# Rounding the transposed probabilities of a wide row tile in one piece instead of two

## The chip, the cores and the metric

The kernel runs on one core of a Trainium2 chip. The metric is the device time of one execution in microseconds. A core has TensorE (PE; its weight loads are the rows PEld), VectorE (DVE), ScalarE (ACT), GpSimd (POOL) and SyncE (SP), each with its own queue of instructions, and they wait for each other by semaphores. PSUM, into which PE writes, has eight banks of 512 fp32 columns.

## What is computed

One transformer layer with attention and a gated feed-forward part side by side, cut to what matters here:

```python
xn = _layernorm(x)                                  # x: 2 x 1024 x 256
q = (xn @ Wq + bq).reshape(b, h, t, dh)             # 16 heads of 128
k = (xn @ Wk + bk).reshape(b, t, h, dh).transpose(0, 2, 3, 1)
v = (xn @ Wv + bv).reshape(b, t, h, dh).transpose(0, 2, 1, 3)
logits = jnp.einsum('bhtd,bhds->bhts', q, k) * scale
mask = jnp.triu(jnp.full((t, t), -jnp.inf, dtype=x.dtype), k=1)
weights = jax.nn.softmax(logits + mask, axis=-1)
out = jnp.einsum('bhts,bhsd->bhtd', weights, v)
attn = out.transpose(0, 2, 1, 3).reshape(b, t, h * dh) @ Wo + bo
result = x + attn + ffn(xn)                         # ffn: 4-bit weights, 2048 wide
```

## The kernel before

All products are made to near fp32 precision from two fp32r parts, a rounded high part and a rest: `split_matmul` (lines 41 to 43) issues three matmuls, high by high, high by low, low by high. So each operand that comes out of PSUM is first rounded by ScalarE (`..._hi`) and then subtracted by VectorE (`..._lo`).

The norm and the feed-forward part come first. Then follows a loop over 256 row tiles `s`: 32 heads (two sequences of 16) times 8 row tiles of 128 queries. By the causal mask row tile `i` of a head has `i + 1` blocks of 128 keys. Its stages are:

- PE: the scores into one of two bank pairs (banks 0-1, 2-3), `scores(s)`.
- DVE, line 858: adds the mask, moves the scores to `probs` and makes the row maximum. ACT, line 420: the exponential. POOL, lines 635 and 638: one over the row sum, and the scaling of `probs`.
- three tiles later (`LAG`), PE, line 1029: transposes the `i + 1` blocks of `probs` into bank 5 or 6, four blocks to a bank. Tiles 4 to 7 are wide: they take two banks, in two chunks. ACT, line 406 (`pt_high`): rounds a chunk into `pt_hi`. DVE, line 770 (`pt_low`): subtracts into `pt_lo`. A head has 12 chunks, which take bank 5 and 6 in turn, and a chunk's transposes wait until the chunk before the last one is subtracted:

```python
wait(pe, pt_lo_done, at - 1)
```

- PE, `with_v`: the product of two row tiles with V, into bank 4, every second step.

Between these stages each step has jobs of K, V and output projections, which all use bank 7 (`M`), one after the other. A job waits until DVE has emptied bank 7 of the job before it (`job_lo_done`): lines 723 (K), 728 (V), 735 (output). For K and V ACT first makes the high part (lines 384, 387). The order is written out in tables, the same for all heads:

```python
FIRST_AT = {0: "K0", 2: "O0a", 6: "O1b", 7: "Vb"}
EARLY_AT = {1: "K1", 3: "O0b", 5: "O1a"}
LATE_AT = {3: "Va"}
```

In step `i` PE does the transposes of the tile three steps back, the FIRST job, the scores of tile `i`, the EARLY job, the product with V where `i` is odd, and the LATE job. So the transposes of tiles 3, 4, 5, 6, 7 of a head stand in steps 6, 7, 0, 1, 2, and those of the next head's tile 0 in step 3. Between the transposes of tile 7 and of tile 0 stand O0a and the scores of tile 2 only; between those of tiles 5 and 6 K0 and the scores of tile 0. DVE does in step `i`: `pt_low` of the tile three back, the FIRST job's evacuation, line 858, the EARLY job's. In step 2 it does O0a's output sum between the two chunks of tile 7. In heads 7, 15 and 23 the steps 2 to 6 also project Q for the next eight heads (`q_step`).

Of the kernel before, what the change touches and what calls it, by code (L numbers as in the profile page):

```python
# [14 lines left out]
ACT = mybir.ActivationFunctionType  # L15
# [3 lines left out]
P = 128  # L19
# [15 lines left out]
def flat(ap):  # L35
    return ap.rearrange("p a b -> p (a b)")
# [9 lines left out]
def wait(eng, sem, count):  # L46

    if count > 0:
        eng.wait_ge(sem, count)
# [6 lines left out]
def attention(nc, sh, d, out):  # L56
# [4 lines left out]
    GROUP = N // (SEQ // HEADS)  # L61
    GROUPS = NH // GROUP
    TILES = SEQ // P
    CHUNKS = 12
    QT = N // P
    QUARTER = 2 * P
    LAG = 3
# [6 lines left out]
    ps, ident = sh["ps"], sh["ident"]  # L74
# [2 lines left out]
    flat_acc = flat(sh["acc"][:])  # L77
    S = [ps[:, 0:2, :], ps[:, 2:4, :]]
    O, M = ps[:, 4, :], ps[:, 7, :]
    T = [ps[:, 5, :], ps[:, 6, :]]  # L80
    D = [ps[:, 4, :], ps[:, 5, :]]
    WT = flat(ps[:, 6:8, :])[:, 0:W6]

    with ExitStack() as c:
# [84 lines left out]
        def job_of(h, name):  # L169

            if name is None:
                return None
            if name[0] == "K":
                return ("K", h + 1, int(name[1])) if h + 1 < NH else None
            if name[0] == "V":
                pair, j = (h + 1) // 2, (0 if h % 2 else 2) + "ab".index(name[1])
                return ("V", pair, j) if pair < NH // 2 else None
            return ("O", h - 1, int(name[1]), "ab".index(name[2])) if h > 0 else None
# [4 lines left out]
        nth = {job: k + 1 for k, job in enumerate(ORDER)}  # L183
        nth_hi = {job: k + 1 for k, job in enumerate(j for j in ORDER if j[0] != "O")}

        chunk_of = lambda i: i if i < QT else 2 * i - QT
        banks_of = lambda i: 1 if i < QT else 2
        chunk_no = lambda s, ch: s // TILES * CHUNKS + chunk_of(s % TILES) + ch
        pt_block = lambda q: 0 if q % 2 == 0 else 6
        new_group = lambda h: h % GROUP == GROUP - 1 and h + 1 < NH  # L190
        q_steps = lambda h, i: Q_AFTER.get(i, ()) if new_group(h) else ()
# [128 lines left out]
        def _(act):  # L320
# [77 lines left out]
            def pt_high(s):  # L398

                i = s % TILES  # L400
                for ch in range(banks_of(i)):
                    at = chunk_no(s, ch)
                    blocks = min(QT, i + 1 - ch * QT)
                    act.wait_ge(pt_done, at + 1)
                    first = pt_block(i // 2) + ch * QT
                    nc.scalar.activation(  # L406
                        pt_hi[:, first:first + blocks, i % 2 * P:(i % 2 + 1) * P],
                        T[at % 2][:, 0:blocks * P].rearrange("p (a b) -> p a b", b=P), ACT.Copy
                    ).then_inc(pt_hi_done, 1)

            def o_high(h, half):
                act.wait_ge(pv_done, 4 * h + 2 * half + 2)
# [239 lines left out]
        def _(dve):  # L652
# [106 lines left out]
                    dve.wait_ge(q_lo_done, 2 * GROUP * o)  # L759
                q_evacuate(o, u)  # L760

            def pt_low(s, ch):

                i = s % TILES
                at = chunk_no(s, ch)
                blocks = min(QT, i + 1 - ch * QT)
                dve.wait_ge(pt_hi_done, at + 1)
                first = pt_block(i // 2) + ch * QT
                where = (slice(None), slice(first, first + blocks), slice(i % 2 * P, (i % 2 + 1) * P))
                nc.vector.tensor_tensor(pt_lo[where], T[at % 2][:, 0:blocks * P].rearrange("p (a b) -> p a b", b=P),  # L770
                                        pt_hi[where].bitcast(F32), ALU.subtract).then_inc(pt_lo_done, 1)

            def o_low(h, half):
# [65 lines left out]
            dve.wait_ge(mask_made, 1)  # L839
            for s in range(NH * TILES):  # L840
                h, i = divmod(s, TILES)
                between = FIRST_AT.get(i) == "O0a"
                if i - 1 in LATE_AT:
                    evacuate(job_of(h, LATE_AT[i - 1]))
                if s >= LAG:
                    pt_low(s - LAG, 0)
                    if between:
                        evacuate(job_of(h, FIRST_AT[i]))
                    if banks_of((s - LAG) % TILES) > 1:
                        pt_low(s - LAG, 1)  # L850
                if not between or s < LAG:
                    evacuate(job_of(h, FIRST_AT.get(i)))
                hurry = EARLY_AT.get(i) == "O1a"
                if hurry:
                    evacuate(job_of(h, EARLY_AT[i]))
                dve.wait_ge(scores_done, s + 1)
                width = (i + 1) * P
                nc.vector.tensor_tensor_reduce(  # L858
                    probs[:, s % 4, 0:width], flat(bank_of("S", h, i))[:, 0:width], mask_row[:, SEQ - width:SEQ],
                    -1.0, -MASKED, ALU.add, ALU.min, neg_max[:, s % 16:s % 16 + 1]).then_inc(max_done, 1)  # L860
                if not hurry:
                    evacuate(job_of(h, EARLY_AT.get(i)))
                if i == 3 and h > 0:
                    o_low(h - 1, 1)
                if i == 7:
                    o_low(h, 0)
                if i == 1 and new_group(h):
                    wq_low((h + 1) // GROUP * HEADS)
                    wq_low((h + 1) // GROUP * HEADS + 1)
                for u in q_steps(h, i):  # L870
                    q_step(h // GROUP + 1, u)

            def pt_lows(s):
                for ch in range(banks_of(s % TILES)):
                    pt_low(s, ch)

            end = NH * TILES
            pt_lows(end - 3)
            evacuate(("O", NH - 1, 0, 0))
            pt_lows(end - 2)  # L880
            evacuate(("O", NH - 1, 0, 1))
            pt_lows(end - 1)
            o_low(NH - 1, 1)
            evacuate(("O", NH - 1, 1, 0))
            evacuate(("O", NH - 1, 1, 1))
# [2 lines left out]
        def _(pe):  # L888
# [130 lines left out]
            def transposes(s):  # L1019
                i = s % TILES  # L1020
                pe.wait_ge(probs_done, s + 1)
                if s == 0:
                    pe.wait_ge(acc_done, STEPS)
                for ch in range(banks_of(i)):
                    at = chunk_no(s, ch)
                    wait(pe, pt_lo_done, at - 1)
                    for n in range(min(QT, i + 1 - ch * QT)):
                        b = ch * QT + n
                        last = nc.tensor.transpose(T[at % 2][:, n * P:(n + 1) * P], probs[:, s % 4, b * P:(b + 1) * P],  # L1029
                                                   ident[:])  # L1030
                    last.then_inc(pt_done, 1)

            def with_v(h, q):

                pe.wait_ge(pt_lo_done, chunk_no(h * TILES + 2 * q + 1, banks_of(2 * q + 1) - 1) + 1)
                pe.wait_ge(job_lo_done, nth[("V", h // 2, q)])
                if q % 2 == 0:
                    wait(pe, o_lo_done, 2 * h + q // 2)
                for s in range(2 * q + 2):
                    first = P if s == 2 * q + 1 else 0  # L1040
                    out_ = O[:, q % 2 * QUARTER + first:(q % 2 + 1) * QUARTER]
                    b = pt_block(q) + s
                    last = split_matmul(nc, out_, v_hi[:, h % VSLOTS, s, :], v_lo[:, h % VSLOTS, s, :],
                                        pt_hi[:, b, first:], pt_lo[:, b, first:], s == 0, s == 2 * q + 1)
                last.then_inc(pv_done, 1)
# [111 lines left out]
```

## Time and profile before

| | |
|---|---|
| median of 3 runs | 1270.23 us (1269.38 to 1271.47) |
| the profiled execution | 1270.06 us |
| its span, first to last instruction | 1268.3 us |
| mean granted TensorE clock | 0.995 |
| PE busy | 1236.2 us (97%), 8306 matmuls |
| PEld busy | 1119.3 us (88%) |
| DVE busy | 876.2 us (69%) |
| ACT busy | 738.6 us (58%) |
| POOL busy | 737.8 us (58%) |
| the transposes, line 1029 | 1152, 172.5 us busy, PE idle before them 2.6 us |
| `pt_hi`, line 406 | 384 operations, 174.2 us busy |
| `pt_lo`, line 770 | 384 operations, 204.0 us busy |

The loop over the heads runs from about 342 us to the end. Busy times are sums over the whole execution. The end of a matmul is modelled, so for PE the starts are the sharper reading. An engine's idle time is charged to what released it.

### The profile page before, as it was taken

The numbers are of one execution on the slowest core, as the hardware profiler recorded it, in microseconds if no ns is written. First come the engines' busy times: TensorE is split into PE (matmuls) and PEld (weight loads), VectorE is DVE, ScalarE is ACT, GpSimd is POOL, SyncE is SP. The second block draws the span as 40 slices with busy tenths as digits, with TensorE's granted clock in tenths as the row PEclk, the third lists the DMA queues.
The fourth block names the chain that finished last, engine by engine and source line by source line (L and its number), as shares of the span: only waits on it lengthen the run. The fifth ranks groups of instructions, "written<-read, shape, count | busy, mean of one in ns | idle before, by whom it ended". The sixth has DMA issues, their size and how long they took to land.

```text
span 1268.3 us, 22067 instructions
## 1 busy us (share of the span) xinstructions
PE 1236.2 (97%) x8306; PEld 1119.3 (88%) x8306; DVE 876.2 (69%) x1694; ACT 738.6 (58%) x1533; POOL 737.8 (58%) x772
## 2 busy tenths in 40 slices
PE   8899999999999999999999999999999999999997
PEld 6688888888899999879999998899999879999996
DVE  7687777776577766667667776677667666677765
ACT  3444444444466666657666675566666656666663
POOL 5574455443376676626666663476775527666663
PEclk9999999999999999999999999999999999999999
DMA  5200000000000000110000002010000100000001
GB/s 143 46 14 13 11 10 14 26 2 9 9 26 13 15 13 18 40 49 13 14 26 5 22 13 72 14 55 13 13 22 10 47 26 14 18 22 7 12 5 34
DMA packets 57337, 29.96 MB, mean 24 GB/s; under 512 B 16272, under 2 KB 57232, under 8 KB 57232
## 3 DMA queue, kind: packets, MB, share of 16 engines
q1 hardware_dynamic: 56016, 27.62, 7.9%
q8 instruction: 68, 1.11, 0.4%
q10 hardware_dynamic: 1216, 0.93, 0.2%
q14 instruction: 37, 0.30, 0.1%
HBM read 26.44 MB, written 2.10 MB: 22 GB/s over the span
## 4 chain that ended last, share of the span: by engine, by line
PE 84%; DVE 5%; ACT 4%; POOL 3%; issue 2%; DMA 1%; SPq 1%; ACTq 0%; POOLq 0%; DVEq 0%
PE ps L41 26%; PE ps L43 25%; PE ps L42 25%; PE ps L1029 8%; DVE k_lo L723 2%; ACT k_hi L384 2%; ACT q_all L335 1%; DMA raw<-in_down 1%; PE ps L922 1%; POOL acc L572 1%; DVE pt_lo L770 0%; POOL codes L551 0%; DVE probs L858 0%; DMA wq_in<-in_wq 0%; POOL w_rows L563 0%
## 5 line engine op out<-in xcount | busy, mean ns | idle before, releaser
L635 POOL TENSOR_TENSOR inv_sum<-row_sum,minus_one 128x1 f32<-128x1 f32 x256 | 141.0, 551 | 309.5 <-ACT probs L420 307.7
L638 POOL TENSOR_TENSOR probs<-probs,inv_sum 128x128 f32<-128x128 f32 (+7 forms) x256 | 296.5, 1158 | 20.0
L770 DVE TENSOR_TENSOR pt_lo<-ps,pt_hi 128x512 fp32r<-128x512 f32 (+3 forms) x384 | 204.0, 552 | 97.5 <-ACT pt_hi L406 97.4
L420 ACT ACTIVATE probs<-probs,neg_max 128x128 f32<-128x128 f32 (+7 forms) x256 | 198.1, 774 | 61.2 <-DVE neg_max L858 58.4
L406 ACT ACTIVATE pt_hi<-ps 128x512 fp32r<-128x512 f32 (+3 forms) x384 | 174.2, 489 | 85.2 <-PE ps L1029 85.2
L858 DVE CUSTOM_DVE_ANT_0 probs<-ps,mask_row 128x128 f32<-128x128 f32 (+7 forms) x256 | 192.1, 751 | 2.6
L42 PE MATMUL ps<-pt_lo,v_hi 128*128 128x256 f32 (+1 forms) x640 | 180.1, 281 | 0.0
L43 PE MATMUL ps<-pt_hi,v_lo 128*128 128x256 f32 (+1 forms) x640 | 180.0, 281 | 0.0
L1029 PE MATMUL ps<-ident,probs 128*128 128x128 f32 x1152 | 172.5, 277 | 2.6 <-DVE pt_lo L770 1.9
L41 PE MATMUL ps<-pt_hi,v_hi 128*128 128x256 f32 (+1 forms) x640 | 173.2, 271 | 1.6 <-DVE pt_lo L770 1.6
L618 POOL TENSOR_TENSOR hid_lo<-act_buf,hid_hi 128x512 fp32r<-128x512 f32 x64 | 82.7, 1293 | 147.0 <-ACT hid_hi L359 147.0
L41 PE MATMUL ps<-k_hi,q_hi 128*128 128x512 f32 (+3 forms) x384 | 140.6, 366 | 0.0
L1029 PEld LDWEIGHTS ps<-ident,probs 128*128 128x128 f32 x1152 | 127.3, 140 | 11.0 <-POOL probs L638 2.8
L43 PE MATMUL ps<-k_hi,q_lo 128*128 128x512 f32 (+3 forms) x384 | 132.9, 346 | 0.0
L42 PE MATMUL ps<-k_lo,q_hi 128*128 128x512 f32 (+3 forms) x384 | 132.7, 346 | 0.0
L41 PEld LDWEIGHTS ps<-pt_hi,v_hi 128*128 128x128 f32 x640 | 121.8, 190 | 4.4 <-DVE pt_lo L770 1.8
L42 PEld LDWEIGHTS ps<-pt_lo,v_hi 128*128 128x128 f32 x640 | 121.8, 190 | 2.7
L43 PEld LDWEIGHTS ps<-pt_hi,v_lo 128*128 128x128 f32 x640 | 122.1, 191 | 0.0
L455 ACT ACTIVATE act_buf<-ps 128x512 f32<-128x512 f32 x64 | 38.4, 599 | 140.4 <-PE ps L43 140.4
L775 DVE SCALAR_TENSOR_TENSOR o_lo<-ps,bv,o_hi 128x512 fp32r<-128x512 f32 x64 | 48.1, 751 | 102.5 <-ACT o_hi L413 102.5
L41 PE MATMUL ps<-xn_hi,w_hi 128*128 128x512 f32 x256 | 103.3, 403 | 0.9 <-DVE w_lo L703 0.4
L42 PE MATMUL ps<-xn_lo,w_hi 128*128 128x512 f32 x256 | 101.8, 398 | 0.0
(105 smaller groups left out, 3211.8 us busy)
## 6 DMA issues: line engine op xcount, KB each, us to landing
wq_in<-in_wq SPq DMA_DIRECT2D x63, 128.0 KB, 2.3
kv_in<-in_wk SPq DMA_DIRECT2D x16, 256.0 KB, 2.8
wo_in<-in_wo SPq DMA_DIRECT2D x32, 128.0 KB, 2.0
kv_in<-in_wv SPq DMA_DIRECT2D x32, 128.0 KB, 2.3
out<-acc SPq DMA_DIRECT2D x8, 256.0 KB, 2.6
acc<-in_x SPq DMA_DIRECT2D x2, 512.0 KB, 5.0
raw<-in_gate SPq DMA_DIRECT2D x16, 64.0 KB, 1.8
raw<-in_up SPq DMA_DIRECT2D x16, 64.0 KB, 2.1
```

The lines of the kernel that those rows point to most:

```text
L41: nc.tensor.matmul(out, w_hi, m_hi, start=start, stop=False)
L42: nc.tensor.matmul(out, w_hi, m_lo, start=False, stop=False)
L43: return nc.tensor.matmul(out, w_lo, m_hi, start=False, stop=stop)
L406: nc.scalar.activation(pt_hi[:, first:first + blocks, i % 2 * P:(i % 2 + 1) * P], T[at % 2][:, 0:blocks * P].rearrange("p (a b) -> p a b", ...
L420: nc.scalar.activation(probs[:, s % 4, 0:width], probs[:, s % 4, 0:width], ACT.Exp, bias=neg_max[:, s % 16:s % 16 + 1], scale=-1.0, accum_ ...
L618: nc.gpsimd.tensor_tensor(hid_lo[:, k % 4, :], act_buf[:, k % 4, :], hid_hi[:, k % 4, :].bitcast(F32), ALU.subtract).then_inc(hid_lo_done, 1)
L635: nc.gpsimd.tensor_tensor(inv_sum[:, at], row_sum[:, at], minus_one[:], ALU.pow).then_inc(inv_done, 1)
L638: nc.gpsimd.tensor_tensor(row, row, inv_sum[:, at].to_broadcast([P, (i + 1) * P]), ALU.mult).then_inc(probs_done, 1)
L770: nc.vector.tensor_tensor(pt_lo[where], T[at % 2][:, 0:blocks * P].rearrange("p (a b) -> p a b", b=P), pt_hi[where].bitcast(F32), ALU.subt ...
L775: nc.vector.scalar_tensor_tensor(o_lo[:], O, bv[:, h % HEADS:h % HEADS + 1], o_hi[:].bitcast(F32), ALU.add, ALU.subtract).then_inc(o_lo_do ...
L858: nc.vector.tensor_tensor_reduce(probs[:, s % 4, 0:width], flat(bank_of("S", h, i))[:, 0:width], mask_row[:, SEQ - width:SEQ], -1.0, -MASK ...
L1029: last = nc.tensor.transpose(T[at % 2][:, n * P:(n + 1) * P], probs[:, s % 4, b * P:(b + 1) * P], ident[:])
```

## The change

A row tile's transposes are one piece. A wide tile fills banks 5 and 6 together, and ScalarE and VectorE each handle its `i + 1` blocks (640 to 1024 columns) in one operation over both banks. A narrow tile takes bank 5 or 6 by the parity of `s`. `pt_done`, `pt_hi_done` and `pt_lo_done` count row tiles instead of chunks. A tile that is wide, or that follows a wide one, waits until the tile before it is subtracted as a whole (`t_free`); the others wait for the tile before that. Nothing else is changed; DVE's sum of O0a, having no place between two chunks any more, follows `pt_low`.

```diff
-    CHUNKS = 12
...
-    T = [ps[:, 5, :], ps[:, 6, :]]
+    T = ps[:, 5:7, :]
...
-        chunk_of = lambda i: i if i < QT else 2 * i - QT
         banks_of = lambda i: 1 if i < QT else 2
-        chunk_no = lambda s, ch: s // TILES * CHUNKS + chunk_of(s % TILES) + ch
+        t_bank = lambda s: flat(T) if banks_of(s % TILES) > 1 else T[:, s % 2, :]
+        t_free = lambda s: s if banks_of(s % TILES) > 1 or banks_of((s - 1) % TILES) > 1 else s - 1
...
             def pt_high(s):
 
                 i = s % TILES
-                for ch in range(banks_of(i)):
-                    at = chunk_no(s, ch)
-                    blocks = min(QT, i + 1 - ch * QT)
-                    act.wait_ge(pt_done, at + 1)
-                    first = pt_block(i // 2) + ch * QT
-                    nc.scalar.activation(
-                        pt_hi[:, first:first + blocks, i % 2 * P:(i % 2 + 1) * P],
-                        T[at % 2][:, 0:blocks * P].rearrange("p (a b) -> p a b", b=P), ACT.Copy
-                    ).then_inc(pt_hi_done, 1)
+                act.wait_ge(pt_done, s + 1)
+                first = pt_block(i // 2)
+                nc.scalar.activation(
+                    pt_hi[:, first:first + i + 1, i % 2 * P:(i % 2 + 1) * P],
+                    t_bank(s)[:, 0:(i + 1) * P].rearrange("p (a b) -> p a b", b=P), ACT.Copy).then_inc(pt_hi_done, 1)
...
-            def pt_low(s, ch):
+            def pt_low(s):
 
                 i = s % TILES
-                at = chunk_no(s, ch)
-                blocks = min(QT, i + 1 - ch * QT)
-                dve.wait_ge(pt_hi_done, at + 1)
-                first = pt_block(i // 2) + ch * QT
-                where = (slice(None), slice(first, first + blocks), slice(i % 2 * P, (i % 2 + 1) * P))
-                nc.vector.tensor_tensor(pt_lo[where], T[at % 2][:, 0:blocks * P].rearrange("p (a b) -> p a b", b=P),
+                dve.wait_ge(pt_hi_done, s + 1)
+                first = pt_block(i // 2)
+                where = (slice(None), slice(first, first + i + 1), slice(i % 2 * P, (i % 2 + 1) * P))
+                nc.vector.tensor_tensor(pt_lo[where], t_bank(s)[:, 0:(i + 1) * P].rearrange("p (a b) -> p a b", b=P),
                                         pt_hi[where].bitcast(F32), ALU.subtract).then_inc(pt_lo_done, 1)
...
-                between = FIRST_AT.get(i) == "O0a"
                 if i - 1 in LATE_AT:
                     evacuate(job_of(h, LATE_AT[i - 1]))
                 if s >= LAG:
-                    pt_low(s - LAG, 0)
-                    if between:
-                        evacuate(job_of(h, FIRST_AT[i]))
-                    if banks_of((s - LAG) % TILES) > 1:
-                        pt_low(s - LAG, 1)
-                if not between or s < LAG:
-                    evacuate(job_of(h, FIRST_AT.get(i)))
+                    pt_low(s - LAG)
+                evacuate(job_of(h, FIRST_AT.get(i)))
...
                 pe.wait_ge(probs_done, s + 1)
                 if s == 0:
                     pe.wait_ge(acc_done, STEPS)
-                for ch in range(banks_of(i)):
-                    at = chunk_no(s, ch)
-                    wait(pe, pt_lo_done, at - 1)
-                    for n in range(min(QT, i + 1 - ch * QT)):
-                        b = ch * QT + n
-                        last = nc.tensor.transpose(T[at % 2][:, n * P:(n + 1) * P], probs[:, s % 4, b * P:(b + 1) * P],
-                                                   ident[:])
-                    last.then_inc(pt_done, 1)
+                wait(pe, pt_lo_done, t_free(s))
+                for b in range(i + 1):
+                    last = nc.tensor.transpose(t_bank(s)[:, b * P:(b + 1) * P], probs[:, s % 4, b * P:(b + 1) * P], ident[:])
+                last.then_inc(pt_done, 1)
 
             def with_v(h, q):
 
-                pe.wait_ge(pt_lo_done, chunk_no(h * TILES + 2 * q + 1, banks_of(2 * q + 1) - 1) + 1)
+                pe.wait_ge(pt_lo_done, h * TILES + 2 * q + 2)
```

The engines' queues show two places. VectorE, steps 1 and 2 of a head: `pt_lo` of tiles 6 and 7, the maxima (line 858) of tiles 1 and 2, `k_lo` of K1, and `acc`, the output sum of O0a. Before:

```order
L770 TENSOR_TENSOR pt_lo<-ps,pt_hi 128x4x128 [waits pt_hi_done]
L770 TENSOR_TENSOR pt_lo<-ps,pt_hi 128x3x128 [waits pt_hi_done]
L858 ISA probs,neg_max<-ps,mask_row 128x256 [waits scores_done]
L858 ISA neg_max 128x1
L723 SCALAR_TENSOR_TENSOR k_lo<-ps,bk,k_hi 128x512 [waits job_hi_done]
L770 TENSOR_TENSOR pt_lo<-ps,pt_hi 128x4x128 [waits pt_hi_done]
L735 TENSOR_TENSOR acc<-ps,acc 128x512 [waits job_done]
L770 TENSOR_TENSOR pt_lo<-ps,pt_hi 128x4x128 [waits pt_hi_done]
L858 ISA probs,neg_max<-ps,mask_row 128x384 [waits scores_done]
```

The same place in the changed kernel (its line numbers are its own):

```order
L763 TENSOR_TENSOR pt_lo<-ps,pt_hi 128x7x128 [waits pt_hi_done]
L845 ISA probs,neg_max<-ps,mask_row 128x256 [waits scores_done]
L845 ISA neg_max 128x1
L718 SCALAR_TENSOR_TENSOR k_lo<-ps,bk,k_hi 128x512 [waits job_hi_done]
L763 TENSOR_TENSOR pt_lo<-ps,pt_hi 128x8x128 [waits pt_hi_done]
L730 TENSOR_TENSOR acc<-ps,acc 128x512 [waits job_done]
L845 ISA probs,neg_max<-ps,mask_row 128x384 [waits scores_done]
```

The pairs are one operation each, and the output sum has moved from between the two halves of tile 7 to behind the whole.

TensorE, steps 2 and 3: the transposes of tile 7, O0a (lines 41 to 43 with `wo`), the scores of tile 2 (with `k`), the transpose of the next head's tile 0, the scores of tile 3. Before:

```order
L1029 MATMUL ps<-ident,probs 128x128 [waits pt_lo_done,probs_done]
L1029 MATMUL ps<-ident,probs 128x128 x3
L1029 MATMUL ps<-ident,probs 128x128 [waits pt_lo_done]
L1029 MATMUL ps<-ident,probs 128x128 x3
L41 MATMUL ps<-wo_hi,o_hi 128x256 [waits o_lo_done,wo_lo_done,job_lo_done]
...
L43 MATMUL ps<-k_hi,q_lo 128x384
L1029 MATMUL ps<-ident,probs 128x128 [waits pt_lo_done,probs_done]
L41 MATMUL ps<-k_hi,q_hi 128x512 [waits max_done]
```

In the changed kernel:

```order
L1009 MATMUL ps<-ident,probs 128x128 [waits pt_lo_done,probs_done]
L1009 MATMUL ps<-ident,probs 128x128 x7
L41 MATMUL ps<-wo_hi,o_hi 128x256 [waits o_lo_done,wo_lo_done,job_lo_done]
...
L43 MATMUL ps<-k_hi,q_lo 128x384
L1009 MATMUL ps<-ident,probs 128x128 [waits pt_lo_done,probs_done]
L41 MATMUL ps<-k_hi,q_hi 128x512 [waits max_done]
```

PE's order is unchanged. The wait in the middle of tile 7 is gone, and the `pt_lo_done` that tile 0 waits for is that of all of tile 7, where it was that of its first four blocks.

## Rows read from the trace of the kernel before

**Rows 1.** Windows: span, busy (x) of PE, PEld, DVE, ACT, POOL; PEclk, DMA, GB/s

```profile
400.00:1250.00 850.00, 839.10 (x5913) 772.18 (x5911) 585.12 (x1190) 548.51 (x1187) 527.32 (x588) 1.00 0.08 22
```

**Rows 2.** The page, chain of work that ended last, shares by engine

```profile
PE 84%; DVE 5%; ACT 4%; POOL 3%; issue 2%; DMA 1%; SPq 1%; ACTq 0%; POOLq 0%; DVEq 0%
```

**Rows 3.** Waits of PEld, 400 to 1250 us: total us, times, longest us

```profile
PEld ps L41 <- DVE k_lo L723: 7.6, 28, 0.3
```

**Rows 4.** Timeline of PE, transposes, two heads: start us, us, engine, line, op, tiles

```profile
602.50 1.06 PE L1029 MATMUL ps<-ident,probs 128*128 128x128 f32 x8
...
604.63 0.30 PE L1029 MATMUL ps<-ident,probs 128*128 128x128 f32 x1
...
628.84 1.06 PE L1029 MATMUL ps<-ident,probs 128*128 128x128 f32 x8
...
630.97 0.30 PE L1029 MATMUL ps<-ident,probs 128*128 128x128 f32 x1
```

**Rows 5.** Timeline of ACT, evacuations of the transposes, same head

```profile
603.16 1.09 ACT L406 ACTIVATE pt_hi<-ps 128x512 fp32r<-128x512 f32 x2 [0.32 <-PE ps L1029]
...
604.96 0.28 ACT L406 ACTIVATE pt_hi<-ps 128x128 fp32r<-128x128 f32 x1 [0.41 <-PE ps L1029]
...
615.02 0.60 ACT L406 ACTIVATE pt_hi<-ps 128x512 fp32r<-128x512 f32 x1 [0.52 <-PE ps L1029]
```

**Rows 6.** Timeline of DVE, the same place

```profile
603.79 0.69 DVE L770 TENSOR_TENSOR pt_lo<-ps,pt_hi 128x512 fp32r<-128x512 f32 x1 [1.70 <-ACT pt_hi L406]
604.40 0.68 DVE L735 TENSOR_TENSOR acc<-ps,acc 128x512 f32<-128x512 f32 x1
```

**Rows 7.** Timeline of PEld and DVE, weight loads, and what the second waited for

```profile
604.60 0.14 PEld L1029 LDWEIGHTS ps<-ident,probs 128*128 128x128 f32 x1
...
625.27 0.19 PEld L41 LDWEIGHTS ps<-xn_hi,kv_hi 128*128 128x128 f32 x1 [0.27 <-DVE k_lo L723]
...
624.47 0.75 DVE L723 SCALAR_TENSOR_TENSOR k_lo<-ps,bk,k_hi 128x512 fp32r<-128x512 f32 x1 [0.38 <-ACT k_hi L384]
```

**Rows 8.** Groups by line and form: ..., xcount | busy us, mean ns | idle before

```profile
L406 ACT ACTIVATE pt_hi<-ps 128x512 fp32r<-128x512 f32 x192 | 111.0, 596 | 53.4 <-PE ps L1029 53.4
...
L406 ACT ACTIVATE pt_hi<-ps 128x128 fp32r<-128x128 f32 x64 | 17.6, 276 | 11.6 <-PE ps L1029 11.6
...
L770 DVE TENSOR_TENSOR pt_lo<-ps,pt_hi 128x512 fp32r<-128x512 f32 x192 | 132.1, 688 | 90.5 <-ACT pt_hi L406 90.5
...
L770 DVE TENSOR_TENSOR pt_lo<-ps,pt_hi 128x128 fp32r<-128x128 f32 x64 | 18.2, 284 | 2.0 <-ACT pt_hi L406 2.0
```

**Rows 9.** Timeline of PE and DVE, transposes of tiles 3 and 4

```profile
614.36 0.62 PE L1029 MATMUL ps<-ident,probs 128*128 128x128 f32 x4
...
616.76 0.71 PE L1029 MATMUL ps<-ident,probs 128*128 128x128 f32 x5
...
615.66 0.69 DVE L770 TENSOR_TENSOR pt_lo<-ps,pt_hi 128x512 fp32r<-128x512 f32 x1 [0.18 <-ACT pt_hi L406]
```

**Rows 10.** Timeline of PE and DVE, transposes of tiles 5 and 6

```profile
621.48 0.84 PE L1029 MATMUL ps<-ident,probs 128*128 128x128 f32 x6
...
623.90 0.96 PE L1029 MATMUL ps<-ident,probs 128*128 128x128 f32 x7
...
623.08 1.01 DVE L770 TENSOR_TENSOR pt_lo<-ps,pt_hi 128x512 fp32r<-128x512 f32 x2
```

**Rows 11.** Timeline of PE, tiles 7 and 0, in a head that also projects Q

```profile
523.76 1.06 PE L1029 MATMUL ps<-ident,probs 128*128 128x128 f32 x8
...
528.68 0.27 PE L1029 MATMUL ps<-ident,probs 128*128 128x128 f32 x1
```

**Rows 12.** Timeline of PE and windows, two idle times and the clock after one

```profile
58.07 1.41 PE L922 MATMUL ps<-ident,w_rows 128*128 128x128 f32 x6 [3.33 <-issue]
...
58.20:61.60 3.40, 3.40 (x12) 2.92 (x12) 1.37 (x3) 0.00 (x0) 1.00 (x1) 0.50 0.00 0
...
539.84 0.50 PE L41 MATMUL ps<-xn_hi,wq_hi 128*128 128x512 f32 x1 [1.23 <-DVE q_all L750]
```

More of the change, by code:

```diff
@@ L871, in _ @@
                     q_step(h // GROUP + 1, u)
-            def pt_lows(s):
-                for ch in range(banks_of(s % TILES)):
-                    pt_low(s, ch)
             end = NH * TILES
-            pt_lows(end - 3)
+            pt_low(end - 3)
             evacuate(("O", NH - 1, 0, 0))
-            pt_lows(end - 2)
+            pt_low(end - 2)
             evacuate(("O", NH - 1, 0, 1))
-            pt_lows(end - 1)
+            pt_low(end - 1)
             o_low(NH - 1, 1)
```

## The prediction

> **What bounds the kernel now.** I read the windows first: between 400 and 1250 us, all of it the loop over the heads, TensorE is busy 839.1 of 850 us at full granted clock, while VectorE has 585, ScalarE 549 and GpSimd 527 [rows 1]. The chain that ended last agrees: 84% of it is PE [rows 2]. So removing work from ScalarE or VectorE shortens nothing by itself, and only some 11 us of 850 are PE waiting. Of these the largest regular piece is K's second half, which waits until VectorE has emptied the first half out of bank 7: 7.6 us in 28 waits [rows 3]. What remains to read is whether PE's new waits end later than PE gets to them. For that I laid the timelines of PE, ACT and DVE over each other at the four places where transposes follow a wide tile, and at the one where a wide tile follows tile 3.
>
> A head takes 26.34 us (628.84 - 602.50, the same row one head later), and the transposes of tile 0 follow those of tile 7 by 2.13 us in both heads [rows 4]. What holds at one head thus repeats at the others.
>
> **Tile 7 to tile 0: the cost.** Before, tile 0's transpose needed only the first four blocks of tile 7 out of bank 5 or 6. ScalarE begins them at 603.16, while PE still transposes the other four [rows 5]; VectorE subtracts them from 603.79 to 604.48 [rows 6]; PE loads the weights of tile 0 at 604.60 [rows 7], straight after the scores and without a wait. Now it needs all eight blocks. Step by step:
> - ScalarE cannot begin before the last transpose. One transpose lets it begin 0.33 us after PE's start (604.96 - 604.63), four let it begin 0.66 us after (615.02 - 614.36) [rows 4, 5, 9]: 0.11 us each. Eight: 0.33 + 7 x 0.11 = 1.10, so 602.50 + 1.10 = 603.60. ScalarE has nothing else then; it idled 0.32 us before 603.16.
> - The rounding of 1024 columns: 128 columns take 276 ns, 512 take 596 [rows 8], so 107 ns per 128 and 276 + 7 x 107 = 1.02 us: until 604.62. VectorE begins 0.03 us behind (603.79 against 603.76): 604.65.
> - The subtraction: 284 and 688 ns [rows 8], 135 ns per 128, 284 + 7 x 135 = 1.23 us: until 605.88.
> - PE's weight load follows such a release by 0.05 us (625.27 against 624.47 + 0.75) [rows 7]: 605.93 against 604.60, a stall of 1.33 us. The first products after a stall also come without weights loaded ahead; I add 0.07, as an estimate. I take **1.40 us**.
>
> Bounds: below, 1.25, if a two-bank operation is a little cheaper than the line through its sizes; above, 1.65, if it costs as two operations end to end (1.09 us on ScalarE, 2 x 0.69 less the overlap on VectorE) plus a full reload.
>
> How often: 31 heads are followed by another. In three of them (before heads 7, 15 and 23) Q's projection of the next group stands between the two tiles, and PE gets to tile 0 4.92 us after tile 7 [rows 11], later than the 3.43 it would now have to wait for. That leaves 28: 28 x 1.40 = **39.2 us** (35 to 46). It lies on PE, and PE is the path.
>
> VectorE's output sum O0a moves behind the whole subtraction, from 604.40 to about 605.8. It frees bank 7 for O0b, at about 606.5; PE gets there after tile 0 and scores 3, at about 606.8. It costs nothing now, but its cover is 0.3 us.
>
> **Tile 5 to tile 6.** Transposes at 621.48 [rows 10], ScalarE from 621.48 + 0.33 + 5 x 0.11 = 622.36, 768 columns 0.81 us, VectorE from 623.20 for 0.96, to 624.16, PE's load at 624.21. Its matmuls began at 623.90, so 0.34 us are lost. But right behind them stands the wait for k_lo, and PE idled 0.27 us there [rows 7]; that wait hangs on K's first half, which PE did before tile 6 and which doesn't move. So 0.07 us remain: 31 x 0.07 = **2.2 us** (0 to 10.5, the latter if nothing is absorbed).
>
> **The other places.** Tile 3 to 4: the new wait is for tile 3's subtraction, over at 616.35; PE comes at 616.76 [rows 9]. Nothing, covered by 0.4 us. Tiles 4 to 5 and 6 to 7 have V's or K's projection between them and, for the latter, an attention product besides; I count nothing. At the ends of the loop there is less between the tiles; behind the last tile 7 the product with V waits for the subtraction directly. By the two stalls above I put **1.5 us** there (0.8 to 2).
>
> **What goes.** 128 operations of ScalarE and of VectorE: their fixed part is 276 - 107 = 169 ns and 284 - 135 = 149 ns, so 21.6 and 19.1 us of busy time. On the path they are worth nothing, since both engines idle before these very groups [rows 8]. The Trainium skill (Perfetto Trace Analysis, Optimizing Scalar/DVE Operations) says that grouping pays "if the engine is saturated", and that where these engines are not saturated but cause bubbles elsewhere, breaking instructions up may let work finish sooner. Here the busy shares say the second case. By the first the time would fall, which is the second rival.
>
> **The sum.** 39.2 + 2.2 + 1.5 = 42.9 us on the profiled execution's 1270.06: **1313 us**. That execution lies 0.17 us under the median of the three runs, so it needs no correction.
>
> **The rivals.**
> 1. More is passed on. O0b's cover of 0.3 us is the thinnest: it is gone if the pair of operations takes 0.3 us more than I say, for O0a's sum stands directly behind them. Another 0.3 us in each of 28 heads is 8.4: 1321; with tile 5's 10.5 less 2.2 on top, 1330. For it: VectorE's queue at this place has no idle time left. Against it: the maxima run three tiles ahead of the transposes.
> 2. Not slower. The fixed costs saved let ScalarE and VectorE empty K's first half earlier, and the wait for k_lo (7.6 us) goes: 1262.5. This needs the subtraction of all eight blocks to be over by 604.55, 0.95 us after the last transpose; two operations in a row of 0.60 and 0.69 us for half the width speak against it. Here also belongs the reading in which grouping as such pays: the 20 us of fixed cost would give 1250.
> 3. Part of the stall is given back, because work of the other engines catches up while PE stands and later waits shrink. All that there is to win back is PE's idle 10.9 us: 1302.
> 4. The clock. After PE had idled 3.33 us, the granted clock was 0.50 for 3.4 us, the lower level of 1.2 GHz; after the 1.23 us idle before 539.84 it stayed at 1.00 [rows 12, 1]. Were each of the 28 stalls followed by such a stretch, it would cost 1.7 us each time: 48 more, 1361. The Trainium skill (TensorE: Matmul & The Clock Gate, A second HAM failure mode) tells of a kernel whose short idles at its PSUM buffers make the clock swing between its two levels, which would be this case. The trace so far speaks against it.
>
> **How the numbers follow.** Forecast as summed 0.75; rival 1 0.11, rival 2 0.03, rival 3 0.07, rival 4 0.04. The forecast's own bounds are 1270 + 35 + 0 + 0.8 = 1306 and 1270 + 46 + 10.5 + 2 = 1328, both ends unlikely together; I keep 1303 to 1326. That leaves out rivals 2, 3 and 4 (0.14), the upper part of rival 1 and the outermost of the forecast. A measurement can tell 0.2% or 2.5 us from no change. Faster has rival 2, 0.03; the same 0.01, for a stall found almost wholly covered; slower 0.96.
>
> **What would show it.** PE should wait on pt_lo some 28 times, 1.3 to 1.4 us each, and a head should take 27.7 to 27.8 us instead of 26.34. Two-bank operations should last 1.02 and 1.23 us. The wait for k_lo should almost vanish, and a wait before tile 6 of about 0.3 us stand in its place. ScalarE and VectorE should show about 20 us less work. The granted clock should stay at 1.00. The prediction is wrong if the head stays within 0.3 us of 26.34, if the stall stands at another pair of tiles, or if the clock falls.

## The result, and the profile after

| | before | changed |
|---|---|---|
| median | 1270.29 us | 1316.13 us |
| profiled execution | 1270.06 us | 1317.51 us |
| its span | 1268.3 us | 1315.7 us |
| `pt_hi` operations, busy | 384, 174.2 us | 256, 167.0 us |
| `pt_lo` operations, busy | 384, 204.0 us | 256, 193.5 us |

The kernel became slower. The ratio of its time to that of before is 1.0352, with a 95% interval of 1.0337 to 1.0366, which is 44.7 us (42.8 to 46.5). One disturbed execution of the changed kernel (and one of the run with scores and O0b ahead of tile 0, below) is left out of the ratio but stands in the median; the other three took 1314.25 to 1317.51 us (there 1283.01 to 1285.32).

First the windows, over the same stretch of the head loop as [rows 1], and over one head (from one tile 7 to the next); the columns are those of [rows 1]:

```profile
400.00:1250.00 850.00, 803.33 (x5661) 738.39 (x5660) 553.07 (x1022) 520.83 (x1022) 502.43 (x559) 1.00 0.08 22
```
```profile
642.90:670.70 27.80, 26.22 (x194) 24.47 (x194) 18.26 (x34) 17.38 (x34) 17.86 (x21) 1.00 0.06 16
```

PE idles 46.7 us of 850 where it idled 10.9, at the same granted clock. A head takes 27.80 us instead of 26.34, and PE is idle in 1.58 of them. The page's chain of work that ended last shows what took PE's share ([rows 2] had PE at 84%, ACT at 4% and DVE at 5%):

```profile
PE 77%; ACT 8%; DVE 8%; issue 3%; POOL 2%; DMA 1%; SPq 1%; ACTq 0%; POOLq 0%; DVEq 0%
PE ps L43 22%; PE ps L42 22%; PE ps L41 22%; PE ps L1009 9%; DVE pt_lo L763 5%; ACT pt_hi L402 4%; ACT o_hi L408 2%; ACT q_all L334 1%; DMA raw<-in_down 1%; PE ps L905 1%; POOL acc L567 1%; DMA wq_in<-in_wq 0%; POOL codes L546 0%; DVE probs L845 0%; POOL w_rows L558 0%
```

`pt_hi` and `pt_lo`, which were hidden, now stand in the chain with 9% of the span. The waits of PE and of its weight loads, 400 to 1250 us:

```profile
PE ps L1009 <- DVE pt_lo L763: 39.1, 52, 1.3
...
PEld ps L1009 <- POOL probs L633: 37.0, 24, 1.5
PEld ps L1009 <- issue: 12.1, 28, 0.4
```

The 52 waits are 24 of 1.25 us before tile 0 and 28 of 0.3 us before tile 6. The second line is the same long wait seen at the weight load. That instruction waits for two semaphores, and the record names POOL's `probs`; but those were scaled 3.3 us before the load, and the matmul's own row names `pt_lo`. The wait for `k_lo` of [rows 3] is no longer in the list.

One head's step 2 and 3, from the timelines of PE, PEld, ACT and DVE, answers to [rows 4 to 7]:

```profile
642.91 1.06 PE L1009 MATMUL ps<-ident,probs 128*128 128x128 f32 x8
...
646.44 0.30 PE L1009 MATMUL ps<-ident,probs 128*128 128x128 f32 x1 [1.26 <-DVE pt_lo L763]
```
```profile
646.40 0.14 PEld L1009 LDWEIGHTS ps<-ident,probs 128*128 128x128 f32 x1 [1.55 <-POOL probs L633]
```
```profile
644.00 1.03 ACT L402 ACTIVATE pt_hi<-ps 128x1024 fp32r<-128x1024 f32 x1 [1.28 <-PE ps L1009]
```
```profile
645.07 1.22 DVE L763 TENSOR_TENSOR pt_lo<-ps,pt_hi 128x1024 fp32r<-128x1024 f32 x1 [2.55 <-ACT pt_hi L402]
646.21 0.68 DVE L730 TENSOR_TENSOR acc<-ps,acc 128x512 f32<-128x512 f32 x1
646.80 0.55 DVE L845 CUSTOM_DVE_ANT_0 probs<-ps,mask_row 128x384 f32<-128x384 f32 x1
```

Measured from the first transpose of tile 7, tile 0 starts 3.53 us after it, where it was 2.13. ScalarE starts 1.09 us after it and works 1.03; VectorE starts 0.04 behind and works 1.22; its end at 646.29 is followed by PE's load 0.11 later.

Tiles 5 and 6 of the next head, where PE waits for the whole of tile 5 ([rows 10] had 2.42 us between them; here it is 2.83):

```profile
663.26 0.84 PE L1009 MATMUL ps<-ident,probs 128*128 128x128 f32 x6
...
666.09 0.96 PE L1009 MATMUL ps<-ident,probs 128*128 128x128 f32 x7 [0.32 <-DVE pt_lo L763]
```

I subtracted, over all heads, the distance between the starts of neighbouring tiles' transposes in the trace of before from that in the trace after. Tile 7 to tile 0 takes 1.40 us more in 28 pairs and 0.0 in the other three, 39.2 us together. Tile 5 to 6 takes 0.41 more in all 32 heads, 13.2 us, and tile 6 to 7 0.33 less in 30 of them, -10.2 us. The other pairs sum to 1.2. Ahead of the loop there are 1.8 us more, and behind the last transposes of tile 7 2.3; both are looked at in the last section.

### The profile page after: what moved, and what is told of

It is laid out like the page before. It is cut to its first block, busy times and chain, and to the rows that moved or that the text cites. A ratio compares the mean times of both kernels' runs of the same rounds, so it can differ in the third digit from the quotient of the medians.

```text
span 1315.7 us, 21811 instructions
## 1 busy us (share of the span) xinstructions
PE 1236.6 (94%) x8306; PEld 1119.6 (85%) x8306; DVE 871.2 (66%) x1566; ACT 734.4 (56%) x1405; POOL 736.8 (56%) x772
## 4 chain that ended last, share of the span: by engine, by line
PE 77%; ACT 8%; DVE 8%; issue 3%; POOL 2%; DMA 1%; SPq 1%; ACTq 0%; POOLq 0%; DVEq 0%
PE ps L43 22%; PE ps L42 22%; PE ps L41 22%; PE ps L1009 9%; DVE pt_lo L763 5%; ACT pt_hi L402 4%; ACT o_hi L408 2%; ACT q_all L334 1%; DMA raw<-in_down 1%; PE ps L905 1%; POOL acc L567 1%; DMA wq_in<-in_wq 0%; POOL codes L546 0%; DVE probs L845 0%; POOL w_rows L558 0%
## 5 line engine op out<-in xcount | busy, mean ns | idle before, releaser
L763 DVE TENSOR_TENSOR pt_lo<-ps,pt_hi 128x128 fp32r<-128x128 f32 (+7 forms) x256 | 193.5, 756 | 141.5 <-ACT pt_hi L402 139.9
L402 ACT ACTIVATE pt_hi<-ps 128x128 fp32r<-128x128 f32 (+7 forms) x256 | 167.0, 652 | 131.1 <-PE ps L1009 130.7
L613 POOL TENSOR_TENSOR hid_lo<-act_buf,hid_hi 128x512 fp32r<-128x512 f32 x64 | 82.7, 1292 | 148.0 <-ACT hid_hi L358 148.0
```

Of the source, the lines that this page charges most:

```text
L402: nc.scalar.activation(pt_hi[:, first:first + i + 1, i % 2 * P:(i % 2 + 1) * P], t_bank(s)[:, 0:(i + 1) * P].rearrange("p (a b) -> p a b", ...
L613: nc.gpsimd.tensor_tensor(hid_lo[:, k % 4, :], act_buf[:, k % 4, :], hid_hi[:, k % 4, :].bitcast(F32), ALU.subtract).then_inc(hid_lo_done, 1)
L763: nc.vector.tensor_tensor(pt_lo[where], t_bank(s)[:, 0:(i + 1) * P].rearrange("p (a b) -> p a b", b=P), pt_hi[where].bitcast(F32), ALU.sub ...
```

## Experiments

The kernels of the experiments have one common form, in which a wide tile can be taken whole or bank by bank, for ScalarE (`HI_WHOLE`) and VectorE (`LO_WHOLE`) apart. With both empty it is the kernel before; the transposes of a bank wait for the subtraction that last read this bank. With all four tiles whole it differs from the changed kernel in one wait: the first four transposes of tile 4 need the subtraction of tile 2, not that of tile 3. Where VectorE takes tile 7 bank by bank, its sum of O0a stays between the two pieces; where it takes it whole, the sum comes behind. The diffs show the lines that differ from run to run.

**Tile 7 back in two pieces.**

```diff
+    HI_WHOLE, LO_WHOLE = (4, 5, 6), (4, 5, 6)
```

> Tiles 4, 5 and 6 in one piece, tile 7 in two as before. Theory (the stall stands between tile 7 and tile 0, 1.40 us in 28 heads): it goes, what is left is 0.07 us behind tile 5 in 31 heads and under 1 us at the ends, so 1273 us (1271 to 1276), and the transposes of tile 0 follow those of tile 7 by 2.13 us again. Rival (every wide tile costs its share, because an operation over two banks is what is slow): a quarter of the 45.8 us goes, 1305 us.

Measured: 1274.29 us, ratio 1.0037 (1.0026 to 1.0047). Of the 45 us all but 4 to 5 are gone with one tile of the four. Tile 0 follows tile 7 at the old distance in every head. What is left in PE's waits for `pt_lo` is tile 6's (window 400 to 1250 us):

```profile
PE ps L1036 <- DVE pt_lo L776: 10.7, 29, 1.7
```

28 of these have the size of 0.3 us, and the pair after each is 0.33 us shorter; the one of 1.7 us, in the last head but one, was 1.3 us in the kernel before. So only 3 us of them stay. The theory holds and the rival, that each wide tile costs a share, falls.

**Tile 7 alone in one piece.**

```diff
+    HI_WHOLE, LO_WHOLE = (7,), (7,)
```

> Tile 7 alone in one piece, tiles 4 to 6 in two. Theory: 28 x 1.40 = 39.2 us over the kernel before and at most 1 us at the end, 1310 us (1308 to 1312). Rival (each wide tile its share): a quarter of the 45.8 us, 1282 us.

Measured: 1312.98 us, ratio 1.0336 (1.0319 to 1.0353), 42.7 us. The sum of the pairs tile 7 to 0 is 39.18 us, 1.4 in each of 28; the rest, 5.3 us, lies ahead of the loop (3.7) and behind it (2.1), less 0.5 elsewhere. The median is 1 us above the bounds that I had set, which left 1 us for the ends. In the waits the old one, for `k_lo`, stands unchanged:

```profile
PE ps L1036 <- DVE pt_lo L776: 32.6, 26, 1.3
...
PEld ps L41 <- DVE k_lo L730: 7.5, 28, 0.3
```

With the run before it, the two parts add up to the whole: 42.7 and 4.7 against 44.7 us, within what the intervals leave open.

**ScalarE whole, VectorE bank by bank.**

```diff
+    HI_WHOLE, LO_WHOLE = (4, 5, 6, 7), ()
```

> ScalarE rounds a wide tile in one operation, VectorE subtracts it bank by bank, and tile 0 waits for the first bank only. Theory (the stall is the sum of ScalarE's late start, its longer operation and VectorE's): PE's weight load of tile 0 comes at 603.60 + 1.02 + 0.03 + 0.69 + 0.05 = 605.39 on the clock of the trace of before, 0.79 us late, with the 0.07 of a restart 0.86 us; 28 heads, 24 us, and under 1 us elsewhere: 1295 us (1292 to 1298). Rival (only VectorE's whole operation holds the bank, ScalarE's part is hidden): 28 x 0.54 = 15 us less than the changed kernel's loss or more, with all of it gone at 1271 us.

Measured: 1297.40 us, ratio 1.0215 (1.0197 to 1.0233), 27 us. In PE's timeline tile 0 comes 3.00 us after tile 7, 0.87 more than before (0.86 expected):

```profile
637.38 1.06 PE L1036 MATMUL ps<-ident,probs 128*128 128x128 f32 x8
...
640.38 0.30 PE L1036 MATMUL ps<-ident,probs 128*128 128x128 f32 x1 [0.73 <-DVE pt_lo L776]
```

So ScalarE's part is not hidden, and over half of the stall comes from it. The 28 pairs sum to 24.3 us, as expected. The 2 to 3 us above 1295 lie at the ends (1.9 ahead of the loop, 0.9 behind it).

**ScalarE bank by bank, VectorE whole.**

```diff
+    HI_WHOLE, LO_WHOLE = (), (4, 5, 6, 7)
```

> ScalarE rounds bank by bank, VectorE subtracts a wide tile in one operation. Theory: ScalarE is done with both banks at 604.25 on the clock of the trace of before, VectorE runs from 604.28 to 605.51, PE loads at 605.56, 0.96 us late and 1.03 with the restart; 28 heads, 29 us, and about 1.5 us elsewhere: 1301 us (1298 to 1304). Rival (the subtraction alone holds the bank): 1316 us, as the changed kernel.

Measured: 1302.86 us, ratio 1.0252 (1.0236 to 1.0268), 32 us; the distance is 3.15 us, 1.02 more than before (1.03 expected):

```profile
637.41 1.06 PE L1036 MATMUL ps<-ident,probs 128*128 128x128 f32 x8
...
640.56 0.30 PE L1036 MATMUL ps<-ident,probs 128*128 128x128 f32 x1 [0.88 <-DVE pt_lo L776]
```

The two do not add up to 1.40, and by the theory they shouldn't. ScalarE whole costs its late start, 603.60 - 603.16 = 0.44, and its longer operation, 0.42. VectorE whole costs its longer operation, 0.54, and the time until ScalarE has done the second bank, 604.25 - 603.76 = 0.49. With both whole it is 0.44 + 0.42 + 0.54 = 1.40; the wait for the second bank is then already contained in ScalarE's part. These three sums are delays of the subtraction's end, and PE is later by the same amounts (0.86, 1.03 and 1.40 against 0.87, 1.02 and 1.40).

**All whole, the scores of tile 3 ahead of tile 0's transpose.**

```diff
+    HI_WHOLE, LO_WHOLE = (4, 5, 6, 7), (4, 5, 6, 7)
...
-                if s >= LAG:
+                late = i in (3,)
+                if s >= LAG and not late:
                     transposes(s - LAG)
                 run(job_of(h, FIRST_AT.get(i)))
                 scores(s)
+                if s >= LAG and late:
+                    transposes(s - LAG)
                 run(job_of(h, EARLY_AT.get(i)))
```

> All wide tiles in one piece; in step 3 PE does the scores of tile 3 before the transpose of tile 0. Theory: the 0.84 us of scores fill the stall, but O0b behind it waits for bank 7, which VectorE empties only behind the whole of tile 7, at about 606.5 on the clock of the trace of before; PE would be there at about 606.1, so 1.1 of the 1.40 us stay: 28 x 0.3 = 8 us less than the changed kernel, about 1307 us. Rival (O0b's wait has cover and the scores fill 0.84 us): 28 x 0.84 = 23.5 us less, 1292 us.

Measured: 1309.49 us, ratio 1.0311 (1.0294 to 1.0329). In every normal head 0.84 us of work were moved into a stall of 1.40, 23.5 us in all, and 6.6 came back by the distances 7 to 0 and 0 to 1 together (8 expected). The stall is shorter, and behind it a new one stands, in the weight loads' waits:

```profile
PEld ps L1036 <- POOL probs L645: 24.0, 25, 1.0
...
PEld ps L41 <- DVE acc L742: 9.9, 25, 0.4
```

`acc` is O0a's output sum: bank 7 comes free only behind tile 7's whole subtraction. That is the cover of 0.3 us that the prediction named; here it is used up. The rival (1292 us) falls.

**All whole, scores and O0b ahead of tile 0, and VectorE's sum of O0a ahead of tile 7's subtraction.** In PE's loop the transposes of step 3 follow the EARLY job too; on VectorE:

```diff
+                first = FIRST_AT.get(i) == "O0a" and s >= LAG
+                if first:
+                    evacuate(job_of(h, FIRST_AT[i]))
                 if s >= LAG:
                     pt_low(s - LAG, 0)
...
-                if not between or s < LAG:
+                if (not between or s < LAG) and not first:
                     evacuate(job_of(h, FIRST_AT.get(i)))
```

> All wide tiles in one piece; in step 3 PE does the scores of tile 3 and O0b before the transpose of tile 0, and VectorE adds O0a's sum before it subtracts tile 7. Theory: some 1.55 us of PE's work now lie between the end of tile 7's transposes and tile 0 in addition, the subtraction ends 0.25 us later than in the changed kernel, at about 606.15, PE comes to tile 0 at 606.2: the 39.2 us are gone, 1273 us (1271 to 1278). Rival (the operations over two banks cost PE something by themselves, or the displaced work makes a new wait): 1290 us or more.

Measured: 1284.18 us, ratio 1.0106 (1.0088 to 1.0123). 31 of the 39 us came back; the forecast of 1273 was 11 us too low, and 1284 lies outside its bounds. Its step on PE was too tight. In the trace the 13 us that stay are 7.6 at this step, 3.1 at tile 6 and 2.3 behind the loop. VectorE and PE, in one head:

```profile
633.00 0.69 DVE L742 TENSOR_TENSOR acc<-ps,acc 128x512 f32<-128x512 f32 x1 [2.21 <-PE ps L43]
633.61 1.21 DVE L776 TENSOR_TENSOR pt_lo<-ps,pt_hi 128x1024 fp32r<-128x1024 f32 x1
```
```profile
634.61 0.28 PE L43 MATMUL ps<-wo_hi,o_lo 128*128 128x256 f32 x1
634.97 0.30 PE L1039 MATMUL ps<-ident,probs 128*128 128x128 f32 x1
```

The subtraction ends at 634.82, 3.62 us after tile 7's start at 631.20, which is what was expected (3.65). But PE had issued all its work 0.17 us earlier than I had put it, and the load came 0.12 us behind the release instead of 0.05. 0.24 us more of waiting, 28 times, is 6.8 us; the pairs 7 to 0 and 0 to 1 together are 7.6 us longer than before. The rival's reading, a lasting cost of operations over two banks, is not needed for it: PE's idle time is all before that one load.

**The kernel before, three matmuls with V ahead of K's second half.** This tests what else the step-1 wait was worth, and is the candidate for a better version.

```diff
                 scores(s)
+                ahead = 1 if i in (1,) and s >= LAG + 2 else 0
+                if ahead:
+                    ph, pi = divmod(s - LAG - 2, TILES)
+                    with_v(ph, pi // 2, 0, ahead)
                 run(job_of(h, EARLY_AT.get(i)))
                 if i % 2 == 1 and s >= LAG + 2:
                     ph, pi = divmod(s - LAG - 2, TILES)
-                    with_v(ph, pi // 2)
+                    with_v(ph, pi // 2, ahead)
```

(`with_v` takes the first and the last of its key blocks; the first block's three matmuls are issued early, and only the last block counts up `pv_done`.)

> The kernel before, with the first three of the 18 matmuls of the product of tiles 4 and 5 with V moved ahead of K's second half in step 1. Theory: they take 0.36 us and fill the 0.27 us that PE waits for k_lo there in every head, and the restart behind it: 0.27 to 0.35 us in some 30 heads, 8 to 10 us less: 1261 us (1259 to 1264). Rival (K's second half ends later and the wait reappears at O0a): 1270 us.

Measured: 1261.53 us, ratio 0.9931 (0.9916 to 0.9946), 8.8 us less than before. The window of one head, which now takes 26.00 us with PE busy in all of it:

```profile
626.30:652.30 26.00, 26.00 (x194) 24.51 (x194) 18.37 (x38) 17.35 (x39) 17.81 (x21) 1.00 0.06 16
```

**All of these together, all tiles whole.** Step 3 as filled above, the scores of tile 1 ahead of tile 6's transposes, and the three matmuls.

```diff
+    HI_WHOLE, LO_WHOLE = (4, 5, 6, 7), (4, 5, 6, 7)
...
-                if s >= LAG:
+                late, last_of = i in (1,), i == 3
+                if s >= LAG and not late and not last_of:
                     transposes(s - LAG)
                 run(job_of(h, FIRST_AT.get(i)))
                 scores(s)
+                if s >= LAG and late:
+                    transposes(s - LAG)
...
                 run(job_of(h, EARLY_AT.get(i)))
+                if s >= LAG and last_of:
+                    transposes(s - LAG)
```

> All wide tiles in one piece, step 3 as in the run with the stall filled, the scores of tile 1 before the transposes of tile 6, and three matmuls with V before K's second half. Theory: no stall of the change is left and the wait for k_lo is gone too: 1264 us (1261 to 1269), that is, like the kernel before with the three matmuls alone plus 1.5 us at the ends; 20 us less work of ScalarE and of VectorE change nothing. Rival (fewer operations are worth something once the stalls are filled): 1255 us or less.

Measured: 1272.77 us, ratio 1.0017 (1.0008 to 1.0026). This lies outside the bounds. The forecast was too low again by the same step: the pairs 7 to 0 and 0 to 1 are 7.6 us longer together, as in the run above. Tiles 5 to 6 and 6 to 7 give back 7.9 us together, 2 us less than the three matmuls alone (9.9), so tile 6's wait is filled all but these 2 us. The rival falls: 128 operations less on each of two engines bring nothing that the times show.

**Tiles 4 and 6 whole.** Behind them the next transposes come latest: those of tile 5 begin 4.7 us after those of tile 4, and those of tile 7 4.9 us after those of tile 6, against 2.4 us from tile 5 to 6 and 2.1 from tile 7 to 0.

```diff
+    HI_WHOLE, LO_WHOLE = (4, 6), (4, 6)
```

> Tiles 4 and 6 in one piece, tiles 5 and 7 in two, else the kernel before. Theory (an operation over two banks costs PE nothing where the next transposes come over 2 us after it): no stall anywhere, 64 operations less on ScalarE and on VectorE, some 10 us less work on each, and the time is that of the kernel before, 1270 us (1268 to 1272). Rival (fewer operations shorten the kernel once they stall nothing): 1265 us or less.

Measured: 1270.20 us, ratio 1.000 (0.9991 to 1.0009). This run doesn't test the 2 us of the expectation: with 4.7 us and more it lies well clear of that bound. The page's busy times:

```profile
PE 1236.8 (97%) x8306; PEld 1119.9 (88%) x8306; DVE 870.0 (69%) x1630; ACT 734.7 (58%) x1469; POOL 736.8 (58%) x772
```

VectorE has 64 operations and 6.2 us less than before, ScalarE 64 and 3.9 less, and the time is the same to 0.1%. (The fixed parts of 64 operations would be 9.5 us on VectorE and 10.8 on ScalarE. The busy time falls by less, since it counts the overlap of two neighbours once: two operations of 0.60 us are one row of 1.09 [rows 5].)

**Tiles 4 and 6 whole, with the three matmuls ahead.**

> Tiles 4 and 6 in one piece, and the first three matmuls with V ahead of K's second half. Theory: as the kernel before with the three matmuls ahead alone, 1261.5 us (1259 to 1264). Rival (the whole tile 6, subtracted 0.26 us later, delays the freeing of bank 7 and gives back part): 1265 us.

Measured: 1261.24 us, ratio 0.9928 (0.9914 to 0.9942), the same as with the three matmuls alone. Both versions beat the kernel before and the changed one; the gain is the matmuls', not the whole tiles'.

## Why the prediction was right

**What bounds.** PE bounds the loop, and the saved fixed cost is worth nothing on the path. The run with tiles 4 and 6 whole shows this directly: 64 operations less on each engine, 0.0% of time. Of the two sentences of the Trainium skill (Perfetto Trace Analysis, Optimizing Scalar/DVE Operations) that the prediction weighed, the second decided: VectorE was busy 65% of the head loop after the change, and its longer instruction held up PE. The 20 us of saved work on each engine that I named as a sign are there only in the sums of single durations (384 and 256 of them: `pt_hi` from 187.9 to 167.0 us, `pt_lo` from 212.1 to 193.5); in the busy times, which count overlaps once, they are 4.2 us on ScalarE and 5.0 on VectorE. That sign was sized wrongly, and no term hung on it.

**Tile 7 to tile 0, 28 x 1.40 = 39.2 us.** Measured 39.2, in 28 heads, none in the three that project Q. Step by step, from tile 7's first transpose: ScalarE at 1.10, measured 1.09; 1.02 us long, measured 1.03; VectorE 0.03 behind, measured 0.04; 1.23 us long, measured 1.22; PE's load 0.05 behind, measured 0.11. The sum at the load came to 1.33, and I added 0.07 for a restart. No run shows a restart: the next matmul, of the scores, starts 0.05 us after tile 0's transpose, as before. What the traces show is a release of 0.11 to 0.12 us, where I had taken 0.05 from the wait for `k_lo`; and the kernel before had the same distance already, 604.60 behind 604.48, in each of the 28 heads. So tile 0's load had no cover at all, and the later end of the subtraction, 605.88 - 604.48 = 1.40, passed on in full. I had read that load as "without a wait", with 0.07 us to spare. The two errors, 0.07 of cover and 0.07 of restart, cancel: the total was right partly by luck. Why a transpose's load comes 0.11 us behind its release and that of K's second half 0.05 stays open. The two runs with one engine whole confirm the rest of the decomposition (0.87 and 1.02 against 0.86 and 1.03), and splitting tile 7 alone removes the stall.

**O0a's sum costs nothing, with 0.3 us of cover.** In the changed kernel PE waits for no `acc`. Once the scores were moved into the stall, the cover was gone and PE waited 9.9 us in 25 weight loads.

**Tile 5 to 6, 0.34 lost and 0.27 given back.** Measured 0.41 and 0.33. The net term, 0.07 in 31 heads and 2.2 us, is measured as 0.08; the pairs sum to 3.0, since tile 6 is late in all 32 heads and the last two heads give only 0.0 and 0.14 back. The release is 0.06 us slower here as well, and so both sides of this term were 0.06 too small.

**Tiles 4 to 5 and 6 to 7: nothing. Tile 3 to 4: nothing.** So in the trace, except once in the first head, where tile 4 comes 0.32 us later. The prediction's row was of another head, with 0.4 us of cover; the first head has less. In the runs with all tiles whole where tile 4 begins without waiting for tile 3, these 0.32 us are absent.

**The ends, 1.5 us.** This is the one mis-sized term: 2.3 us behind the last transposes of tile 7, in the profiled execution. 0.8 of them are the longer wait, 1.5 the lower clock of the last section, which the term did not contain. Before it, tile 6 of the last head loses another 0.3, counted above.

**The rivals.** More passed on: not seen; no later wait was added. Not slower: no. Given back by later waits: only at `k_lo`, as the sum had it. The clock: at 1.00 through the loop, with idle times of 1.26 us in 28 heads, so the swing that the Trainium skill (TensorE: Matmul & The Clock Gate, A second HAM failure mode) tells of is not seen here; where the clock did fall is told below. The predicted 42.9 us stand 2 us under the 44.7 of the ratio. Between the two profiled executions the difference is 47.4 us, 4.5 more than predicted: 1.8 ahead of the loop, in a part that the change does not touch, 0.8 more at the end, 0.8 more at tile 6, and 1.2 in the other pairs.

## What to carry to other kernels

An operation that empties two buffers at once holds both until it ends, starts only when both are full, and passes its whole length on to the next engine in the chain. Lay the next writer's arrival beside it, both counted from the first write. Here the merged buffers came free 3.5 us after tile 7's first transpose and 2.8 us after tile 5's: where the next transposes were due at 4.7 us or later, the merged operation was free, and where they were due at 2.1 or 2.4 us, it delayed them by the difference every time. What of the delay stays depends on the waits behind it: of tile 6's 0.41 us all but 0.08 were won back at `k_lo`. Fixed costs saved on engines that already wait are worth nothing: 64 operations less on each of two engines were worth 0.0%, while three matmuls moved ahead of PE's own wait of 0.27 us were worth 0.7%.

## What the hardware showed unexpectedly

The granted clock fell at both ends for longer than before. Ahead of the loop PE waits for the weights of the feed-forward part (`w_rows`, which GpSimd unpacks), 3.33 us before and 3.70 in the changed kernel's profile. In the trace of before the clock was at 0.50 for the 3.4 us after it [rows 12] and then at 1.00; here it was still at 0.50 (1.2 GHz) in the next stretch, and the matmuls of 512 columns started 0.43 us apart instead of 0.23:

```profile
57.00:61.00 4.00, 2.04 (x8) 1.98 (x9) 2.76 (x5) 0.63 (x1) 3.10 (x3) 0.57 0.00 0
61.20:64.30 3.10, 3.10 (x9) 2.42 (x8) 0.00 (x0) 0.00 (x0) 0.00 (x0) 0.50 0.00 0
```

That is half of the 1.8 us ahead of the loop: PE comes out of this wait 0.9 us later than before already (58.96 against 58.07), and 0.9 come in the longer stretch at the lower level. The code is the same in all kernels here, and it is no work of the change: the loop's first transpose is at 344.5 us in the trace of before, at 346.3 in the changed kernel's, and anywhere from 344.8 to 348.2 in those of the ten experiments. At the end the last product with V follows an idle time of 2.37 us, and it ran at about half clock, where before it ran at full:

```profile
1302.83 0.38 PE L41 MATMUL ps<-pt_hi,v_hi 128*128 128x256 f32 x1 [2.37 <-DVE pt_lo L763]
```
```profile
1303.80:1307.00 3.20, 3.20 (x18) 3.20 (x17) 0.00 (x0) 0.00 (x0) 0.00 (x0) 0.53 0.00 0
```

The same product in the kernel before, from its timeline and its windows:

```profile
1256.88 0.39 PE L41 MATMUL ps<-pt_hi,v_hi 128*128 128x256 f32 x1 [1.57 <-DVE pt_lo L770]
```
```profile
1257.00:1260.00 3.00, 2.94 (x24) 2.79 (x24) 0.00 (x0) 0.02 (x1) 0.00 (x0) 1.00 0.00 0
```

The idle time there was 1.57 us before. The experiments' traces tell the idle time and the clock apart. In the run with all changes together tile 7 is whole as well, and the same product follows the same idle time of 2.37 us, but at full clock:

```profile
1259.89 0.38 PE L41 MATMUL ps<-pt_hi,v_hi 128*128 128x256 f32 x1 [2.37 <-DVE pt_lo L776]
```
```profile
1260.90:1262.70 1.80, 1.80 (x18) 1.80 (x16) 0.00 (x0) 0.00 (x0) 0.00 (x0) 1.00 0.00 0
```

There the part behind tile 7's last transposes is 0.8 us longer than before, all of it the wait, where in the changed kernel it is 2.3. So some 1.5 us are the clock's. The run with ScalarE whole idles 2.44 us at this place and stays at full clock too, while three other runs with 2.4 us idle (tile 7 alone whole, the scores ahead of tile 0, the scores and O0b ahead of tile 0) fall to the lower level as the changed kernel does. A wait of 1.26 us repeated in 28 heads did not lower the clock; one of 2.4 us at the end was followed by the lower level in four of six traces. The idle time alone thus doesn't decide it, and what does stays open.
